# Decay matrices from exponentials of summed logarithms instead of scans, and a reordered pipeline, in a two-layer gated-delta kernel

## The chip, the cores and the metric

One core of a Trainium2 chip. Times are device microseconds of one execution; "before" was timed three times. The profile is of one more execution. TensorE does the matrix products and transposes, VectorE, ScalarE and GpSimd the elementwise work, and SyncE issues most of the DMAs. A pass of TensorE over f32 operands appears in the profile as two instruction records for one call in the kernel.

## The reference

Input: 8 sequences of 256 tokens with 128 features, f32. Layer 0 is a gated delta rule (16 value heads and 8 key heads of width 64) and a mixture of experts, layer 1 an attention and a mixture of experts. The change is in the first half of layer 0. Per sequence it computes (x is the normalised input):

```
mixed = silu(causal_conv4(x @ W_qkv.T));  q, k, v = split(mixed)      # q scaled by 1/8
z     = x @ W_z.T
beta  = sigmoid(x @ W_b.T)
g     = -exp(A_log) * softplus(x @ W_a.T + dt_bias)                    # log of the decay
for each token t, per head:
    S = S * exp(g_t)
    S = S + k_t (v_t - k_t S) beta_t
    o_t = q_t S
h = o * silu(z);  h = h * rsqrt(mean(h*h) + 1e-6) * norm_weight;  y = h @ W_out.T
```

The kernel works in chunks of 128 tokens. In a chunk the recurrence is a triangular system. Its matrix entry for the tokens i and j is (k_i . k_j) times beta times the product of the decays between them, so for each head and chunk a 128 x 128 matrix D of beta times products of decays is needed, 32 of them in a sequence.

## The kernel before, in words

The first layer runs as a software pipeline over `it` from -2 to 7. In one turn sequence f = it + 2 is normalised, projected and convolved; sequence n = it + 1 gets its matrices D, its products and the inverse of its triangular matrices; sequence i = it gets solutions, outputs, states, the norm of the heads and the output projection. Each engine's order is written out by hand in a loop of its own; engines wait on semaphores, and a queue never overtakes. After it comes a loop over four pairs of sequences for the rest (the mixture of experts and the second layer), which the diff does not touch apart from where the constants lie.

What the change touches:

- **D by scans.** `decays` (ScalarE, line 560) takes exponentials of the log decays. `decay_rows` (TensorE, line 950) spreads the decays of four heads along the rows of a PSUM bank, `diagonal` (GpSimd, line 454) puts beta on the diagonal of `dm`, and `scan` (VectorE, line 1586) multiplies and adds along 512 columns, so that `dm` becomes D. Batch k = 0 to 7 is four heads of one chunk. `w_last` copies D's last column.
- **Products.** `key_products` (TensorE, line 965) writes k.k and k.q of a batch to bank 2, and `products` (VectorE, lines 1604 and 1608) multiply them by D. The next batch's key products wait for `pt_ready` of the one before.
- **Decay to the chunk's end.** `turn_decay`, `gamma`, `turn_gamma` and `gamma_tokens` make the product of the decays from the chunk's start by a transpose, a scan and a transpose back.
- **Softplus.** `exponents` and `log_decays` (VectorE, lines 1534 to 1577) compute the log decay by a polynomial, in three parts. Beta is made by two instructions of its own from the same exponential.
- **The inverse.** `diagonal_blocks` (ScalarE, line 602) gathers the 32-row blocks, `invert` (VectorE, lines 1627 to 1641) inverts them in 30 steps of two instructions each, and then turns the result twice (1639 and 1641). TensorE merges the blocks to 64 rows and to 128 (`solve32`, `merge32`, lines 999 to 1015; `solve64`, line 1025; `merge64`, line 1038), with copies on ScalarE between them (lines 608 to 648).
- **Projection and convolution.** `project` (TensorE, line 935) computes a pair of channel tiles into banks 3 and 4 in turns, `seed` (ScalarE, line 571) starts the convolution of it, `convolve` (VectorE, line 1522) does six instructions, `silu` (ScalarE, line 580) ends it. A bank is free for the next pair but one when its convolution is done.
- **Gates.** `gate` (TensorE, line 920, ScalarE, line 668) computes z of sequence i and its Silu between the solutions and the outputs of that sequence.
- **Solutions, outputs, states.** `solve` (line 1057), `outputs` (line 1069), `end_state`, `from_state` (line 1090) on TensorE; `take_state`, `query_state`, `gated` on VectorE.
- **Norm of the heads.** `squares` (ScalarE, line 682), `sum_squares` (VectorE, lines 1664 and 1666), `root_of_squares` (GpSimd, line 468), `normalise` (VectorE, line 1670), then `turn_heads` (line 1106) and `project_out` (line 1118) on TensorE.

## Time and profile before

| | |
|---|---|
| median of three runs | 1913.48 us (1912.42 to 1915.88) |
| the profiled execution's own time | 1893.33 us |
| its span, first to last instruction | 1891.5 us |
| busy: TensorE, VectorE, ScalarE, GpSimd | 1473.5, 1000.2, 658.6, 196.7 us |
| mean granted clock of TensorE | 0.782 of full |
| sequence pipeline of layer 0 | to about 1037 us |

Engines overlap, so the busy times do not add up to the span. A share of busy time alone does not say which engine a stage waits for; for that the profile is cut into stretches. TensorE's granted clock has two levels here, 1.0 (2.4 GHz) and 0.5 (1.2 GHz); a mean between them says how much of the stretch was at either. The sections of the profile name engines in short: PE is TensorE, DVE VectorE, ACT ScalarE, POOL GpSimd.

### The profile page before, as it was taken

Reading aid. Unit: us, or ns where it says so; the run is one execution under the profiler, and the core shown is the slowest. Engines: PE = TensorE matmul, PEld = TensorE weight load, DVE = VectorE, ACT = ScalarE, POOL = GpSimd, SP = SyncE. Lnnn points to the kernel's source line nnn. Section 1 sums busy time; section 2 is a strip of 40 time slices with the busy share of each in tenths; the row PEclk is TensorE's granted clock in tenths of the full one; section 3 lists DMA queues with packets and bytes.
Section 4 is the critical chain, followed back from the end, with each engine's and each line's share of the span. In section 5 each row is a group of like instructions: output and inputs, shape, how many; then the busy total and the mean of one; then the engine's idle time right before and its main releaser. Section 6 shows DMA issues by size and latency. Waiting matters only on the chain.

```text
span 1891.5 us, 28271 instructions
## 1 busy us (share of the span) xinstructions
PE 1473.5 (78%) x11320; PEld 1115.6 (59%) x11328; DVE 1000.2 (53%) x2493; ACT 658.6 (35%) x1089; POOL 196.7 (10%) x189
## 2 busy tenths in 40 slices
PE   2759599597794995958857877897869977897879
PEld 1547487476674774757756554665547654566446
DVE  5866765867668567676742462225331452235421
ACT  1433252342522533425332413342333423342332
POOL 5010030200201202002001000000010000000010
PEclk8658667687586675966958877898789977898879
DMA  3000000000000000000003000000000000000000
GB/s 98 3 1 4 0 10 1 1 9 1 2 9 1 10 1 1 7 1 26 1 1 131 1 7 1 1 7 6 2 0 1 7 6 1 1 6 1 1 1 6
DMA packets 15078, 17.77 MB, mean 9 GB/s; under 512 B 2567, under 2 KB 13344, under 8 KB 14560
## 3 DMA queue, kind: packets, MB, share of 16 engines
q1 hardware_dynamic: 12768, 14.03, 2.2%
q8 instruction: 93, 1.52, 0.3%
q0 software_dynamic: 576, 1.76, 0.3%
q10 hardware_dynamic: 1600, 0.12, 0.1%
q14 instruction: 41, 0.34, 0.1%
HBM read 13.81 MB, written 2.10 MB: 8 GB/s over the span
## 4 chain that ended last, share of the span: by engine, by line
PE 41%; issue 29%; DVE 23%; ACT 3%; POOL 2%; DMA 1%; SPq 0%; DVEq 0%; POOLq 0%; ACTq 0%
DVE arena L1632 4%; DVE arena L1635 4%; PE ps L1069 4%; PE ps L1440 4%; PE ps L1449 3%; PE ps L965 3%; PE ps L935 3%; PE ps L1025 3%; PE ps L1038 3%; DVE arena L1522 3%; PE ps L950 2%; PE ps L920 2%; PE ps L1057 1%; PE ps L999 1%; PE ps L1257 1%
## 5 line engine op out<-in xcount | busy, mean ns | idle before, releaser
L1522 DVE SCALAR_TENSOR_TENSOR arena<-ps,conv_w,arena 128x255 f32<-128x255 f32 (+2 forms) x384 | 166.0, 476 | 108.0 <-ACT arena L571 103.4
L999 PE MATMUL ps<-arena 32*32 32x32 f32 x512 | 28.9, 236 | 156.7 <-DVE arena L1639 156.7
L1449 PEld LDWEIGHTS ps<-arena 128*128 128x128 f32 x1152 | 133.7, 192 | 15.3 <-issue 14.6
L1440 PE MATMUL ps<-arena 128*128 128x512 f32 x288 | 139.6, 633 | 0.0
L1449 PE MATMUL ps<-arena 128*128 128x128 f32 x1152 | 133.8, 275 | 0.0
L858 ACT ACTIVATE arena<-ps 128x512 f32<-128x512 f32 x144 | 86.0, 597 | 132.2 <-PE ps L1440 132.1
L1586 DVE TENSOR_TENSOR_SCAN arena<-ps,arena 128x512 f32<-128x512 f32 x64 | 78.1, 1220 | 99.2 <-PE ps L950 99.2
L999 PEld LDWEIGHTS ps<-arena 32*32 32x32 f32 x512 | 27.9, 151 | 158.5 <-DVE arena L1639 158.5
L935 PE MATMUL ps<-arena 128*128 128x256 f32 x256 | 104.0, 554 | 21.9 <-DVE arena L1522 21.3
L1930 DVE SCALAR_TENSOR_TENSOR arena<-ps,rw,arena 128x128 f32<-128x128 f32 x128 | 36.0, 344 | 139.0 <-PE ps L1449 139.0
L468 POOL TENSOR_TENSOR o_rstd<-ssq,half_power 128x16 f32<-128x16 f32 x16 | 46.4, 2901 | 562.9 <-DVE ssq L1666 562.9
L965 PE MATMUL ps<-arena 64*128 64x256 f32 x256 | 88.0, 473 | 17.4 <-DVE arena L1608 17.4
L494 POOL TENSOR_TENSOR rstd<-var_eps,half_power 128x2 f32<-128x2 f32 (+1 forms) x28 | 23.3, 833 | 746.6 <-DVE var_eps L1493 746.6
L1440 PEld LDWEIGHTS ps<-arena 128*128 128x128 f32 x288 | 56.4, 205 | 60.0 <-issue 59.0
L935 PEld LDWEIGHTS ps<-arena 128*128 128x128 f32 x256 | 64.6, 277 | 41.9 <-DVE arena L1522 28.7
L1635 DVE TENSOR_TENSOR arena<-arena 128x30 f32<-128x30 f32 (+14 forms) x240 | 79.7, 332 | 8.2
L1632 DVE TENSOR_TENSOR arena<-arena 128x30 f32<-128x30 f32 (+14 forms) x240 | 79.6, 332 | 8.2
L1069 PEld LDWEIGHTS ps<-arena 128*128 128x128 f32 x512 | 79.5, 248 | 5.2 <-issue 5.2
L1069 PE MATMUL ps<-arena 128*128 128x64 f32 x512 | 80.4, 332 | 0.0
L950 PE MATMUL ps<-con,decay 128*128 128x128 f32 x512 | 78.0, 304 | 2.8 <-DVE arena L1586 2.8
L950 PEld LDWEIGHTS ps<-con,decay 128*128 128x128 f32 x512 | 71.2, 212 | 10.6 <-issue 5.2
L1235 PE MATMUL ps<-con,h_tok 128*128 128x128 f32 x48 | 13.4, 434 | 82.0 <-DVE h_tok L1499 82.0
(247 smaller groups left out, 3139.3 us busy)
## 6 DMA issues: line engine op xcount, KB each, us to landing
arena<-in_routed_up SPq DMA_DIRECT2D x1, 2048.0 KB, 9.7
arena<-in_routed_down SPq DMA_DIRECT2D x1, 2048.0 KB, 14.7
x_ln<-in_x SPq DMA_DIRECT2D x8, 128.0 KB, 2.1
arena<-in_w_mix SPq DMA_DIRECT2D x1, 1024.0 KB, 10.4
x_in<-in_x SPq DMA_DIRECT2D x8, 128.0 KB, 2.6
out_x<-x_res SPq DMA_DIRECT2D x8, 128.0 KB, 1.9
arena<-out_x SPq DMA_DIRECT2D x4, 256.0 KB, 2.8
out_x<-arena SPq DMA_DIRECT2D x4, 256.0 KB, 2.7
```

The lines of the kernel that those rows point to most:

```text
L858: act.activation(hid1[e % 2][:, i, :], ps[:, i, :], ACT.Gelu).then_inc(s["mgelu"], 1)
L935: mm = pe.matmul(ps[:, 4 - p % 2, j * SEQ:(j + 1) * SEQ], w_mix[:, m * P:(m + 1) * P], hT3[:, f % 3, :], start=True, stop=True)
L950: mm = pe.matmul(ps[:, k % 2, h * P:(h + 1) * P], decay[n % 2][:, c, v:v + 1].to_broadcast([P, P]), ident0, start=True, stop=True)
L965: mm = pe.matmul(ps[:, 2, 2 * P * g:2 * P * (g + 1)].rearrange("p (q n) -> p q n", q=2), mix_qk[n % 2][r:r + DH, QK_TILES + m, cs], mix_qk ...
L999: pe.matmul(ps[32:64, c, BLOCK * h:BLOCK * (h + 1)], at[0:32, v, 32:64], tt[0:32, v, 0:32], start=True, stop=True)
L1069: mm = pe.matmul(ps[:, (7, 5)[g], h * DH:(h + 1) * DH], dm[i % 2][:, VH * c + v, :], eps[:, v, :], start=True, stop=True)
L1440: pe.matmul(ps[:, i, :], m_up[:, e, i * P:(i + 1) * P], hT, start=True, stop=True)\
L1449: mm = pe.matmul(ps[:, 4 + e % 2, c * P:(c + 1) * P], hid1[e % 2][:, i, c * P:(c + 1) * P], m_down[:, e, i, :], start=(i == 0), stop=(i == ...
L1522: ins = dve.scalar_tensor_tensor(conv_tile(f, m)[:, sh:SEQ], ps[:, 4 - p % 2, j * SEQ:(j + 1) * SEQ - sh], conv_w[:, m, TAPS - 1 - sh:TAPS ...
L1586: dve.tensor_tensor_scan(d, ps[:, k % 2, :], d, 0.0, ALU.mult, ALU.add).then_inc(s["scan_done"], 1)
L1632: me.did(dve.tensor_tensor(tmp, inv[:, j + 1:BLOCK, j:j + 1].to_broadcast([P, rows, j]), inv[:, j:j + 1, 0:j].to_broadcast([P, rows, j]), ...
L1635: me.did(dve.tensor_tensor(inv[:, j + 1:BLOCK, 0:j], inv[:, j + 1:BLOCK, 0:j], tmp, ALU.add))
```

## The change

Each matrix D is now the exponential of a sum of logarithms. `masked_decays` (GpSimd) multiplies the log decays of four heads into an upper triangle of ones. `decay_sums` (TensorE) puts the causal mask of large negative numbers into a PSUM bank with a bf16 matmul and adds the sums of the log decays with one f32 matmul of 512 columns. `decay_matrix` (ScalarE) takes the exponential of the bank, one instruction for each head, with the logarithm of beta as its per-partition bias, and writes D. The logarithm of beta comes from the same polynomial as softplus, whose tiles are twice as wide. The decay to the chunk's ends comes from three small matmuls (`chunk_ends`) and one exponential. Signs change in places, since D now has beta positive.

The order of every engine changes too. Five pairs are projected before the inverse ends, into banks 0 to 4. The gates move to the end of the turn and are computed for sequence n in bank 2. The second solve and outputs come after the last key products. The inverse is cut into three parts, with the gated outputs and a sum of squares between them. The first sum of squares and its normalise stand next to each other.

```diff
-                pool.tensor_tensor(dm[f % 2][:, BATCH * k:BATCH * (k + 1), :], over_heads(ident, BATCH),
-                                   over_last(beta[:, c, BATCH * b:BATCH * (b + 1)], P), ALU.mult)\
+                pool.tensor_tensor(gm[k % NB].rearrange("p (h n) -> p h n", h=BATCH), over_heads(upto, BATCH),
+                                   over_last(log_decay[n % 2][:, c, BATCH * b:BATCH * (b + 1)], P), ALU.mult)\
...
+            def decay_matrix(n, k):
...
+                act.wait_ge(s["sum_psum"], CH * NB * n + k + 1)
+                for h in range(BATCH):
+                    v = BATCH * b + h
+                    ins = act.activation(dm[n % 2][:, BATCH * k + h, :], ps[:, k % 2, h * P:(h + 1) * P], ACT.Exp,
+                                         bias=log_beta[n % 2][:, c, v:v + 1])
+                ins.then_inc(s["dm_ready"], 1)
...
-                for h in range(BATCH):
-                    v = BATCH * b + h
-                    mm = pe.matmul(ps[:, k % 2, h * P:(h + 1) * P], decay[n % 2][:, c, v:v + 1].to_broadcast([P, P]), ident0,
-                                   start=True, stop=True)
+            def decay_sums(n, k):
+                if k < 2:
+                    pe.wait_ge(s["conv_done"], NP * n + k + 1)
+                else:
+                    pe.wait_ge(s["dm_ready"], CH * NB * n + k - 1)
+                pe.matmul(ps[:, k % 2, :].rearrange("p (h n) -> p h n", h=BATCH), causal_bf[:, 0, :],
+                          over_heads(ident_bf[:, :], BATCH), start=True, stop=False, skip_group_check=True)
+                pe.wait_ge(s["gm_ready"], CH * NB * n + k + 1)
+                pe.matmul(ps[:, k % 2, :], beyond, gm[k % NB], start=False, stop=True, skip_group_check=True)\
+                    .then_inc(s["sum_psum"], 1)
...
+PAIR_BANK = (0, 1, 2, 4, 3, 4, 3, 4)
...
+                if p >= 5:
                     pe.wait_ge(s["conv_done"], NP * f + p - 1)
...
-                dve.tensor_tensor_scan(d, ps[:, k % 2, :], d, 0.0, ALU.mult, ALU.add).then_inc(s["scan_done"], 1)
...
+            for bank in LEVEL32:
+                for h in range(BATCH):
+                    pe.transpose(ps[:, bank, h * P:(h + 1) * P], ident, ident)
```

VectorE's order after the sixth batch of products, before and after (each name is one call above; i, n and f as in the text):

```diff
-  scan 7, products 6, sum_squares(i, 0), log_decays 1, products 7, gamma_tokens, log_decays 2,
-  normalise(i, 0), gated(i, 1, 0), gated(i, 1, 1), invert(n), sum_squares(i, 1), residual(i, 0),
-  convolve 0, 1, normalise(i, 1), convolve 2 to 6, residual(i, 1), convolve 7
+  log_decays 1, products 6, products 7, log_decays 2, sum_squares(i, 0), normalise(i, 0),
+  inverse steps to 13, gated(i, 1, 0), gated(i, 1, 1), steps 14 to 22, sum_squares(i, 1),
+  steps 23 to 30, turned_inverse, residual(i, 0),
+  convolve 0, 1, normalise(i, 1), convolve 2 to 6, residual(i, 1), convolve 7
```

TensorE's order from the last key products on, after the change: solve(i, 1), outputs(i, 1), the v and k transposes, turn_heads(i, 0), project 0 to 4, project_out(i, 0), solve32 and merge32, solve64 of two groups, project 5, solve64 of two groups, merge64, project 6, two of merge64, project 7, merge64, gate, decay_sums 0 and 1 of f, gate, turn_heads(i, 1), gate, project_out(i, 1), gate. ScalarE's queue ends with the gates' last two Silus, then the Silus of the four v pairs, and begins the next turn with decay_matrix 0 and 1.

## Rows read from the trace of the kernel before

**Rows 1.** The page's first line.

```profile
span 1891.5 us, 28271 instructions
```

**Rows 2.** Stretches by iteration; busy us of each engine (instructions), TensorE clock, DMA share, GB/s.

```profile
114.70:235.10 120.40, 92.22 (x813) 77.09 (x813) 82.69 (x190) 44.93 (x76) 14.00 (x14) 0.68 0.01 2
...
483.80:606.50 122.70, 94.64 (x836) 79.52 (x836) 85.90 (x196) 45.97 (x78) 17.77 (x15) 0.71 0.02 4
...
732.90:855.50 122.60, 94.64 (x836) 79.64 (x836) 85.87 (x196) 45.96 (x78) 17.76 (x15) 0.71 0.01 3
855.50:965.40 109.90, 83.04 (x822) 70.56 (x822) 80.55 (x165) 42.58 (x70) 17.14 (x14) 0.76 0.04 12
```

**Rows 3.** Stretches inside the iteration from 483.8 us: two cuts, same columns.

```profile
483.80:527.40 43.60, 41.53 (x556) 36.92 (x556) 29.41 (x66) 27.42 (x46) 14.83 (x14) 0.66 0.03 8
527.40:575.20 47.80, 44.09 (x232) 35.09 (x232) 27.53 (x56) 9.97 (x16) 2.94 (x2) 0.78 0.01 4
575.20:606.50 31.30, 9.03 (x48) 7.51 (x48) 28.96 (x78) 8.58 (x17) 0.00 (x0) 0.66 0.00 0
...
483.80:512.50 28.70, 28.62 (x468) 25.58 (x469) 17.76 (x36) 17.64 (x28) 11.87 (x9) 0.50 0.01 2
...
556.90:580.30 23.40, 20.85 (x82) 17.83 (x83) 12.59 (x31) 5.37 (x11) 2.90 (x1) 0.51 0.00 1
```

**Rows 4.** Waits from 483.8 to 606.5 us: total, times, longest.

```profile
DVE arena L1522 <- ACT arena L571: 13.3, 4, 4.6
```

**Rows 5.** Timeline of VectorE: start us, duration us, instruction.

```profile
483.71 1.89 DVE L1641 STREAM_TRANSPOSE arena<-arena 128x1024 f32<-128x1024 f32 x1
486.97 5.26 DVE L1522 SCALAR_TENSOR_TENSOR arena<-ps,conv_w,arena 128x255 f32<-128x255 f32 x12
524.27 1.22 DVE L1586 TENSOR_TENSOR_SCAN arena<-ps,arena 128x512 f32<-128x512 f32 x1
566.13 1.21 DVE L1664 TENSOR_REDUCE ssq<-arena 128x16 f32<-128x1024 f32 x1
576.53 1.22 DVE L1670 TENSOR_TENSOR arena<-arena,o_rstd 128x1024 f32<-128x1024 f32 x1
```

**Rows 6.** ScalarE's groups by form in the second layer: busy us, mean ns.

```profile
L858 ACT ACTIVATE arena<-ps 128x512 f32<-128x512 f32 x144 | 86.0, 597 | 132.2 <-PE ps L1440 132.1
L850 ACT ACTIVATE arena<-ps,a_b 128x512 f32<-128x512 f32 x16 | 11.0, 687 | 14.8 <-PE ps L1421 14.8
L814 ACT ACTIVATE arena<-ps 128x128 f32<-128x128 f32 x16 | 4.4, 278 | 18.3 <-PE ps L1292 18.3
```

**Rows 7.** Timeline of TensorE in the second layer, a bf16 matmul.

```profile
1754.72 0.63 PE L1321 MATMUL ps<-causal_bf,ident_bf 128*128 128x512 bf16 x1
```

**Rows 8.** Chain that ended last, TensorE's longest pieces: start, us, line, records.

```profile
491.04 2.00 PE ps L935 x4
493.05 5.31 PE ps L1025 x48
512.81 1.11 PE ps L935 x4
529.83 3.29 PE ps L920 x4
557.48 3.60 PE ps L1057 x16
564.89 7.02 PE ps L1069 x32
```

**Rows 9.** Line 468, the power: duration ns min/median/max, first and last start.

```profile
L468 POOL TENSOR_TENSOR o_rstd<-ssq,half_power x16: 2900/2901/2902, 196.1 to 1024.7; 128x16 f32<-128x16 f32 x16
```

**Rows 10.** Timeline of ScalarE around a load of the exponential table.

```profile
549.48 1.28 ACT L555 ACT_TABLE_LOAD   x1
550.78 0.26 ACT L555 ACTIVATE exp_out<-exp_in 128x64 f32<-128x64 f32 x1
```

**Rows 11.** Line 1560, the polynomial's steps: duration ns min/median/max.

```profile
L1560 DVE SCALAR_TENSOR_TENSOR sp_p<-sp_p,sp_z x48: 191/193/979, 27.4 to 818.3; 128x32 f32<-128x32 f32 x48
```

More of the change, by code:

```diff
@@ L479, in _ @@
                         weighted(i, b)
+                if has_n:
+                    for k in range(5, CH * NB):
+                        masked_decays(n, k)
+                if has_i:
                     root_of_squares(i, 0)
@@ L729, in _ @@
                     turned_heads(i, 0, 1)
+                if has_f:
+                    for p in range(5):
+                        seed(f, p)
+                if has_i:
                     squares(i, 1)
@@ L1064, in outputs @@
                     pe.wait_ge(s["e_ready"], 4 * i + 2 * c + g + 1)
+                    if c == 0 and g == 0:
+                        after(pe, "x_updated", CH * i)
                     if c == 1 and g == 0:
@@ L1719, in _ @@
                 if has_n:
-                    scan(me, n, 4)
                     products(me, n, 3)
```

511 lines of the change are left out of this document (250 added, 261 removed).

## The prediction

> **What bounds the kernel.** I read the page first: the profiled execution has a span of 1891.5 us [rows 1] and its own time is 1893.3 us, 20 us below the median of the three timed runs (1913.5 us). I sum differences in the profiled execution and take them off the median. The table of stretches cuts the first layer at the point where VectorE ends the transpose that releases the 32-row solve (line 1639). From the first such point (114.7 us) to the seventh (855.5 us) there are six full iterations, 123.5 us each, and one of 109.9 us that has no front part [rows 2]. Everything after about 1037 us is the second layer, which the diff leaves alone.
>
> No engine is full in the iteration from 483.8 to 606.5 us: TensorE is busy 94.6 us of 122.7, VectorE 85.9, ScalarE 46.0 [rows 2]. So I cut it into stages [rows 3]. Stage A (483.8 to 527.4, 43.6 us, to the first product of the next sequence) is TensorE's: busy 41.5 us, and its clock stands at the lower level (1.2 GHz, 0.50 of full) for the first 28.7 us. VectorE waits there 13.3 us, four times, for the projection and seed of the next pair [rows 4]. Stage B (527.4 to 575.2, 47.8 us, the eight batches of scans and products) is TensorE's too, busy 44.1 us, the stretch from 556.9 at half clock. Stage C (575.2 to 606.5, 31.3 us) is VectorE's inverse: VectorE 29.0 us busy, TensorE 9.0. The change fills the TensorE hole in C, which costs nothing now, and adds to VectorE there, where it costs.
>
> **The change, stage B.** The eight scans (1.22 us each [rows 5]) leave VectorE, but VectorE has slack in B (27.5 us of 47.8 [rows 3]); ScalarE's 32 exponentials replace them. Price of one: a 128-wide ACTIVATE from PSUM is 278 ns, a per-partition bias adds 90 ns (687 against 597) [rows 6], so 0.37 us; I let neighbours overlap by 0.1 us, which gives 1.2 us a batch, between 1.1 and 1.5 (no overlap). That is 9.6 us more on ScalarE, busy 10.0 us of 47.8: it fits. On TensorE a batch of decay rows (512 f32 columns) becomes 512 bf16 columns and 512 f32 columns; the f32 part is even and the bf16 part is 0.2 us, bounded by nothing and by the 0.63 us of such an instruction alone [rows 7]: six batches in B give +1.3 us. What leaves B counts more: the four gates (3.3 us for two, and two at 1.1), the second solve (3.6 us at half clock for one half, 1.8 for the other) and the second outputs (7.0 us) [rows 8], together 17.9 us, go after the last product or into stage A. One wait is new: products 6 and 7 stand next to each other and the key products share a bank, so the last one waits a product and two thirds of the softplus polynomial behind it, 2.8 us. B = 47.8 - 17.9 + 1.3 + 2.8 = 34.0 us. Bounds: with all of B at full clock 30 us; with a stretch of 24 us at half clock in it about 41.5 us.
>
> **Stage C.** On VectorE, from the last product to the released transpose, both sums of squares are now inside (the first was ahead of product 7, the second after the transpose): 2 x 1.3 us (reduce 1.21 [rows 5] and its scaling). The first is followed at once by the normalise, which needs GpSimd's power, 2.90 us [rows 9]; nothing stands between them, so VectorE waits 3.0 us and with it the inverse that is queued behind. Before, product 7 and the last decay steps covered this. Twice as wide log operations and two more settles: 0.3 us. C = 31.3 + 2.6 + 3.0 + 0.3 = 37.2 us. TensorE's second solve, outputs, transposes and five projections lie beside it: some 22 us at full and 33 us with half of it at the low clock, against 30 us until VectorE asks for the second squares (which ScalarE has queued behind the seeds of pairs 0 to 4). So nothing, up to 4 us if slow; I take nothing.
>
> **Stage A**, counted from the released transpose. VectorE turns the inverse back (1.9), adds one residual (0.3), convolves pairs 0 and 1 (5.26 for two), normalises (1.2) and convolves pairs 2 and 3 [rows 5]: 13.9 us. This is good: four conv waits are gone, since five pairs were projected early. But TensorE, after the 32-row blocks (7.2 us, the start of the first projection at 491.04) and two 64-row groups (5.31 us for three, so 1.77 each at half clock) [rows 8], is ready at 10.8 and its projection of pair 5 waits for pair 3's convolution: 3.1 us lost. Then 2.0 (pair 5), five groups (8.85) and two projections (4.0) bring it to 28.8; the last group and the first gate (2.0) to 32.6. I let the clock rise there, against 28.7 us before, as the wide matmuls come later. Then at full clock two decay sums (2.6), three gates (3.3), the heads' two transposes (2.2) and the output projection (2.2): 42.9. The next sequence's exponential comes later still, since ScalarE's queue holds in front of it the last gate's Silu (0.7), the four v Silus (2.3), which in the old order ran beside the convolutions, and a table load (1.28 [rows 10]); with the first batch of exponentials (1.2) this is 48.5 us. Before, it was 43.6: A = +4.9. VectorE has then been idle since about 34. If TensorE stays at half clock through A it is 57; if it is full from 20 us on it is near 43.
>
> **Sum.** 48.5 + 34.0 + 37.2 = 119.7 against 122.7: -3.0 us, six times -18. The iteration without a front part ran its middle at full clock already, so I give it nothing; likewise the last. In the start-up, the polynomial's six steps took up to 979 ns against 193 [rows 11] while GpSimd multiplied its diagonals; these multiplies now come after it: -6 us with their neighbours. Eight added identity transposes (half clock, 0.5 each, 1.5 of 4 hidden) and wider operations give 3 back, the rest of the start-up -1: -4 us. Together -22 us: 1913.5 - 22 = 1891.5, so 1892 us.
>
> **Two rules of the Trainium skill against it.** The load of the exponential table at 549.48 has no idle time of ScalarE before it, and the exponential starts 1.30 us after it began [rows 10]. The Trainium skill, ScalarE: Activation LUTs, section "What ACT_TABLE_LOAD costs", puts a drain of about 1.38 us beside the load's 1.28 us. By this rule A's queue would be 1.4 us longer in seven iterations, an estimate of 10 us from that page and 1902 us in all; the trace has no such gap. The Trainium skill, SBUF — State Buffer, section "Who interferes with whom", says that a VectorE instruction with two SBUF inputs and a GpSimd one that reads SBUF exclude each other; the 979 ns row agrees, and it is why GpSimd's multiplies 5 to 7, now in the front, could block state updates there. By it each block would cost up to 0.8 us, an estimate from the same row; by my order of the queues they meet products, which read PSUM, and I count nothing.
>
> **Rivals.** (1) The forecast: 0.40. Own range 1878 to 1905, almost all of it faster by over 0.2%.
> (2) The front stays at full clock: B 30.5 us, an iteration 116.2, 6 x -6.5 - 4 = -43: 1870 us. For it: the iteration without front part was at clock 0.76 over all, the others 0.68 to 0.71 [rows 2], with nearly the same front; the short solves leave the front. Against: pieces of half clock have come in all six. 0.24.
> (3) Slower: the stretch of half clock that begins at 556.9 now, mostly under work that moves to C, falls into the front. B is then 41.5, C 39.2 through the late squares, the iteration 129.2, +6.5 us. In four of six iterations: 26 - 6 - 4 = +16: 1930 us. It decides from B = 37.7 us, that is about 17 us of half clock in the front; before it was 20 of 47.8 [rows 3]. TensorE pays here because A has also grown: the front starts 5 us later. 0.26.
> (4) The gain in B is eaten exactly by the waits in C and A, so that the reorder does nothing (within 4 us of 1913.5). 0.06.
> (5) The drain rule above, 1902 us: 0.02, since the trace speaks against it.
> (6) TensorE idles in A as I wrote, but the clock rises early (A 43): 1860 us. 0.02.
>
> 0.2% (4 us) is about what this kernel's runs can tell from no change. Faster by more: 0.38 of (1) gives 0.36, (2) 0.24, and 0.01 of the rest, 0.61. Within: 0.08. Slower: 0.31. The range takes in (2), the clock bounds of A and B, and (3) at five of six: 1852 to 1940.
>
> **What the profile after should show.** Iterations of about 120 us. VectorE: no scan; a 3.0 us gap before the first normalise that waits for GpSimd's power; four conv waits of before gone, but 12 to 15 us idle between the last convolution and the first product, ended by ScalarE's exponential. TensorE: busy over 20 us of stage C, where it was 9.0; one gap of about 3 us before pair 5. ScalarE: batches of four ACTIVATEs of about 0.37 us, one table load between the last v Silu and the first of them. Start-up: first release near 110 us instead of 114.7. I am wrong if B is above 38 us, if a batch takes over 1.5 us, if the power's wait is hidden, or if TensorE's granted clock in A and B together moves by more than 0.1.

## The result and the profile after

The kernel after takes 1846.13 us (median of four runs, 1841.42 to 1851.51) against 1912.95 us for the kernel before on the same chip, a ratio of 0.9653 with the interval 0.9619 to 0.9687. That is 67 us less where the forecast had 22 less. The direction and most of the waits came as forecast; the size did not, and the time lies 6 us below the range. The profiled execution took 1841.42 us, against 1893.33 us for the profiled one of before, which lay 20 us below its own median; so the two traces differ by 52 us only. The loop behind the first layer, which the change leaves alone, also differs by chance: from TensorE's first instruction in it on (L1227 before, L1269 after) it took 846 us in the trace of before and 860 in that of after. So differences are compared stage by stage here.

The page's first line of the kernel after.

```profile
span 1839.6 us, 27803 instructions
```

The table of stretches of the kernel after, cut at the same release points as [rows 2] (VectorE ends the transpose that lets the 32-row solve go, here line 1654). Columns as there: length, busy time of TensorE, its weight loads, VectorE, ScalarE and GpSimd with instructions in brackets, then TensorE's clock.

```profile
105.60:221.30 115.70, 95.83 (x776) 76.01 (x776) 73.75 (x177) 53.85 (x108) 17.01 (x15) 0.69 0.01 2
...
562.10:674.70 112.60, 93.30 (x800) 75.09 (x800) 74.87 (x180) 54.56 (x110) 17.01 (x15) 0.71 0.02 5
...
787.30:895.20 107.90, 87.06 (x774) 69.52 (x774) 69.29 (x150) 50.14 (x98) 16.98 (x14) 0.71 0.04 12
```

From 105.6 to 787.3 us there are six full iterations, 113.6 us each in the mean, where before had 123.5. The first two took 115.6 us, the last four 112.6; where the iterations of a kernel repeat like these four they are called steady here. Six times 9.9 is 59 us. VectorE has 11 us less to do in an iteration and ScalarE 9 more; TensorE's busy time is only 1.3 us less than in [rows 2].

The same view for the stages of the iteration from 562.1 us, A, B and C as in [rows 3], and then for the parts of A and B at either clock level.

```profile
562.10:608.18 46.08, 42.80 (x533) 33.99 (x534) 24.51 (x60) 28.45 (x48) 5.78 (x6) 0.63 0.03 7
608.18:637.86 29.68, 26.43 (x148) 18.58 (x147) 18.87 (x41) 13.77 (x40) 5.40 (x7) 0.93 0.02 6
637.86:674.73 36.87, 24.07 (x123) 22.52 (x122) 31.52 (x82) 12.35 (x24) 5.83 (x2) 0.64 0.00 0
562.10:596.40 34.30, 31.80 (x466) 25.97 (x467) 20.89 (x46) 21.08 (x33) 4.08 (x4) 0.50 0.01 2
596.40:634.00 37.60, 34.03 (x203) 24.04 (x201) 20.80 (x51) 20.58 (x53) 7.11 (x9) 1.00 0.04 11
634.00:637.86 3.86, 3.39 (x11) 2.56 (x11) 1.70 (x4) 0.56 (x1) 0.00 (x0) 0.50 0.02 4
634.00:654.50 20.50, 20.03 (x88) 18.59 (x89) 14.33 (x38) 6.06 (x10) 2.90 (x1) 0.50 0.00 1
```

Against [rows 3], A grew by 2.5 us, B shrank by 18.1 and C grew by 5.5. The second stretch at half clock (1.2 GHz) starts 71.9 us behind the release point and lasts 20.5 us, but B is over at 75.8; 3.9 us of it fall on B. Before, the stretch began at 73.7 us (the 556.9 of [rows 3] is 0.6 us early) and took 17.7 us of B. B also held a short one of 3.4 us, which the steady iterations of after do not have:

```profile
530.20:533.60 3.40, 3.40 (x8) 1.54 (x7) 1.46 (x4) 1.04 (x2) 0.00 (x0) 0.50 0.14 41
557.50:575.20 17.70, 17.45 (x68) 15.04 (x68) 7.13 (x18) 1.13 (x2) 2.90 (x1) 0.50 0.00 1
```

The waits of the iteration from 562.1 us of the kernel after (waiting engine and line, who released it: total us, times, longest).

```profile
DVE x_res L1694 <- PE ps L1166: 13.9, 1, 13.9
PE ps L1038 <- DVE arena L1654: 12.1, 1, 12.1
...
PE ps L1002 <- DVE arena L1634: 3.3, 1, 3.3
...
DVE arena L1686 <- POOL o_rstd L472: 3.0, 1, 3.0
...
PE ps L971 <- DVE arena L1564: 1.1, 1, 1.1
```

The first normalise waits 3.0 us for GpSimd's power, the last key product 3.3 us for products 6, and pair 5 only 1.1 us. VectorE is idle for 13.9 us in A, but ahead of its last residual; the last convolution is queued behind that. TensorE still has a hole of 12.1 us in front of the 32-row solve.

The timeline of ScalarE at the end of A (start us, duration us, instruction).

```profile
602.95 0.60 ACT L691 ACTIVATE arena<-ps 128x512 f32<-128x512 f32 x1 [2.17 <-PE ps L951]
603.45 2.19 ACT L602 ACTIVATE arena<-arena 128x512 f32<-128x512 f32 x4
605.66 1.28 ACT L572 ACT_TABLE_LOAD   x1
606.95 2.17 ACT L572 ACTIVATE arena<-ps,log_beta 128x128 f32<-128x128 f32 x8
```

The last gate's Silu, the four v Silus, the table load and the exponentials follow one another without a gap, and the first product starts at 608.18. The groups of the same iteration by form give the exponential's price.

```profile
L572 ACT ACTIVATE arena<-ps,log_beta 128x128 f32<-128x128 f32 x32 | 9.1, 381 | 5.2 <-PE ps L986 5.2
```

The start-up has its step too: the row of the polynomial, now twice as wide, takes its 0.22 us every time, where [rows 11] had up to 979 ns.

```profile
L1599 DVE SCALAR_TENSOR_TENSOR sp_p<-sp_p,sp_z x48: 224/225/226, 26.6 to 745.6; 128x64 f32<-128x64 f32 x48
```

### The profile page after: what moved, and what is told of

It is laid out like the page before. It is cut to its first block, busy times and chain, and to the rows that moved or that the text cites. A ratio compares the mean times of both kernels' runs of the same rounds, so it can differ in the third digit from the quotient of the medians.

```text
span 1839.6 us, 27803 instructions
## 1 busy us (share of the span) xinstructions
PE 1487.5 (81%) x11040; PEld 1097.3 (60%) x11048; DVE 909.1 (49%) x2365; ACT 730.9 (40%) x1347; POOL 193.3 (11%) x188
## 4 chain that ended last, share of the span: by engine, by line
PE 37%; issue 30%; DVE 25%; ACT 4%; POOL 3%; DMA 1%; SPq 0%; POOLq 0%; DVEq 0%; ACTq 0%
DVE arena L1564 5%; DVE arena L1645 4%; DVE arena L1648 4%; PE ps L1482 4%; PE ps L1491 3%; PE ps L1078 3%; PE ps L1002 3%; PE ps L986 3%; PE ps L971 2%; PE ps L1098 2%; PE ps L951 2%; PE ps L1112 2%; PE ps L1065 2%; PE ps L1463 1%; PE ps L1299 1%
## 5 line engine op out<-in xcount | busy, mean ns | idle before, releaser
L1491 PEld LDWEIGHTS ps<-arena 128*128 128x128 f32 x1152 | 133.7, 192 | 15.3 <-issue 14.6
L1482 PE MATMUL ps<-arena 128*128 128x512 f32 x288 | 135.3, 616 | 0.0
L971 PE MATMUL ps<-arena 128*128 128x256 f32 x256 | 89.0, 505 | 22.0 <-DVE arena L1564 21.3
L1002 PE MATMUL ps<-arena 64*128 64x256 f32 x256 | 79.4, 434 | 30.4 <-DVE arena L1634 24.8
L1002 PEld LDWEIGHTS ps<-arena 64*128 64x128 f32 x256 | 46.7, 203 | 83.0 <-DVE arena L1634 41.5
L1632 DVE TENSOR_TENSOR arena<-ps,arena 128x512 f32<-128x512 f32 x64 | 44.1, 690 | 105.3 <-PE ps L1002 76.3
L1098 PEld LDWEIGHTS ps<-arena 128*128 128x128 f32 x512 | 87.9, 271 | 7.6 <-issue 7.2
L1098 PE MATMUL ps<-arena 128*128 128x64 f32 x512 | 90.4, 359 | 0.2 <-DVE arena L1706 0.2
L572 ACT ACTIVATE arena<-ps,log_beta 128x128 f32<-128x128 f32 x256 | 72.4, 377 | 42.5 <-PE ps L986 42.2
L1482 PEld LDWEIGHTS ps<-arena 128*128 128x128 f32 x288 | 55.0, 200 | 57.0 <-issue 57.0
L1112 PE MATMUL ps<-arena 128*128 128x64 f32 x512 | 86.5, 349 | 0.0
L1112 PEld LDWEIGHTS ps<-arena 128*128 128x128 f32 x512 | 84.8, 262 | 2.3 <-issue 2.3
```

Source lines behind the costliest of these rows:

```text
L572: ins = act.activation(dm[n % 2][:, BATCH * k + h, :], ps[:, k % 2, h * P:(h + 1) * P], ACT.Exp, bias=log_beta[n % 2][:, c, v:v + 1])
L971: mm = pe.matmul(ps[:, PAIR_BANK[p], j * SEQ:(j + 1) * SEQ], w_mix[:, m * P:(m + 1) * P], hT3[:, f % 3, :], start=True, stop=True)
L1002: mm = pe.matmul(ps[:, 2, 2 * P * g:2 * P * (g + 1)].rearrange("p (q n) -> p q n", q=2), mix_qk[n % 2][r:r + DH, QK_TILES + m, cs], mix_qk ...
L1098: mm = pe.matmul(ps[:, 5 + g, h * DH:(h + 1) * DH], um[:, VH * c + v, :], v_tok[:, c, v, :], start=True, stop=True)
L1112: mm = pe.matmul(ps[:, (7, 5)[g], h * DH:(h + 1) * DH], dm[i % 2][:, VH * c + v, :], eps[:, v, :], start=True, stop=True)
L1482: pe.matmul(ps[:, i, :], m_up[:, e, i * P:(i + 1) * P], hT, start=True, stop=True)\
```

## The experiments

Fifteen kernels were run behind it, one of them the kernel after once more. The ratio is to the kernel before on the same chip. The ratios carry 0.3 to 0.9% to either side, so the mean length of the six full iterations in the trace (release point to release point) is what the theories are judged by. That mean has a spread of its own: the kernel after gave 113.6 us in one trace and 112.6 in the other, since a short stretch at half clock, 40 to 51 us behind the release point, lengthens some iterations by about 3 us, two of six in the first trace and one in the second. So a difference of 1 us between means shows nothing. A, B and C are those of the steady iterations, in us.

```
kernel                 ratio (interval)          iteration   A          B          C
before                 1                         123.5       42.8-45.9  46.3-49.2  31.3
after                  0.9653 (0.9619, 0.9687)   113.6       46.1       29.7       36.8
order_alone            0.9736 (0.9649, 0.9824)   115.1       45.2-46.5  31.8-35.1  36.7
filler_before_products 0.9767 (0.9688, 0.9847)   115.2       45.0-46.6  32.4-35.3  36.8
late_pairs             0.9701 (0.9610, 0.9791)   112.1       42.7       32.9       36.9
power_hidden           0.9583 (0.9501, 0.9664)   109.4       46.0       29.7       33.6
keep_busy              0.9663 (0.9583, 0.9742)   112.3       46.1       29.7       36.9
silus_early            0.9654 (0.9585, 0.9723)   112.7       44.0       31.7       36.9
power_silus_keep       0.9582 (0.9503, 0.9661)   111.0       44.0       31.7-35.0  33.6
before_keep_busy       1.0058 (1.0021, 1.0096)   123.3       42.8-45.4  45.8-49.2  31.3
solve_in_front         0.9771 (0.9724, 0.9817)   115.6       46.5       32.7       36.8
power_gates            0.9475 (0.9433, 0.9516)   109.5       43.8       28.8       36.8
power_gates_silus      0.9495 (0.9454, 0.9536)   108.8       41.3       31.2       36.7
after_again            0.9619 (0.9572, 0.9666)   112.6       46.1       29.7       36.8
before_solve_late      0.9657 (0.9601, 0.9713)   112.3       43.8-44.8  37.3       31.1
power_gates_squares    0.9375 (0.9338, 0.9412)   106.1       43.3-44.3  28.7-29.3  33.6
all_squares            0.9388 (0.9352, 0.9425)   106.4       41.1-41.9  30.8-31.4  33.6
```

**order_alone.** The new order of all engines, with the scans, the diagonals and the decay transposes of before in place of the exponentials.

```diff
-                    decay_sums(n, 2)
+                    decay_rows(n, 2)
...
-                    decay_matrix(n, 2)
...
+                    scan(me, n, 2)
                     products(me, n, 2)
```

> The changed kernel's order of all engines, with the scans, GpSimd's diagonals and the decay transposes of the kernel before in place of the exponentials. Theory 1 (the reorder makes the gain: the gates, the second solve and the second outputs leave TensorE's front, and the stretch of half clock then falls where TensorE is not waited for; VectorE has room for scans): an iteration of 114 to 117 us, in all 1850 to 1875 us. Theory 2 (the scans, 8 times 1.22 us, are the gain, since 9.8 us is what an iteration lost): 121 to 123 us an iteration, in all 1900 to 1915 us.

The first line of the diff is TensorE's, the next ScalarE's, the last VectorE's; it is the same for every batch. By the means the order has 8.4 of the 9.9 us per iteration and the exponentials 1.5; against the repeat of after it is 2.5, and the steady iterations are 115.0 to 117.0 us here against 112.6. Theory 1 holds; the exponentials' share lies between 1.5 and 4 us and is not known better.

**filler_before_products.** The kernel after with a reduce of 1.2 us, whose result nobody reads, on VectorE before each of the eight products.

```diff
+                me.did(dve.tensor_reduce(filler[:, :], w_out[:, :, :].rearrange("p m (a d) -> p (m a) d", d=DH), X_AXIS, ALU.add))
                 dve.wait_ge(s["kk_psum"], CH * NB * n + k + 1)
```

> The changed kernel with one reduce of 1.2 us on VectorE ahead of each batch of products (its result is not used), so that VectorE has the scans' time back and nothing else changes. Theory 1 (VectorE waits for TensorE in the front and can hide most of it): iteration 114 to 118 us, stage B at most 34 us. Theory 2 (VectorE's time is the path): iteration 122 us, stage B 39 us.

Some 9.8 us of VectorE's time put back cost 1.6 us of the iteration by the means, 2.6 against the repeat of after. Most of VectorE's load in the front is free, in agreement with order_alone.

**late_pairs.** Pairs 2 to 4 projected and seeded between the inverse's merges, as before the change.

```diff
-                    for p in range(5):
+                    for p in range(2):
                         project(f, p, n, has_n)
...
                     merge32(n, 1)
+                    project(f, 2, n, has_n)
                     solve64(i, n, 0, 0, has_i)
+                    project(f, 3, n, has_n)
                     solve64(i, n, 0, 1, has_i)
+                    project(f, 4, n, has_n)
```

These are TensorE's lines; ScalarE's seeds of the three pairs move with them.

> The changed kernel with pairs 2, 3 and 4 projected and seeded after the inverse again, between the blocks' solves. Theory 1: stage A grows by TensorE's three projections at half clock, 6 us, and by renewed waits for seeds; iteration 118 to 121 us, stage C unchanged. Rival (early projection gains nothing because TensorE's tail is bound by the last gates and VectorE is idle 14 us there anyway): iteration 113 to 115 us.

Theory 1 missed: the iteration is not longer. Two stretches of this kernel in A, from 10 to 18 and 18 to 26 us behind a release point at 333.9 us:

```profile
344.00:352.00 8.00, 8.00 (x42) 5.99 (x41) 5.23 (x12) 5.14 (x9) 0.48 (x1) 0.50 0.00 0
352.00:360.00 8.00, 8.00 (x89) 6.69 (x88) 5.13 (x12) 5.84 (x10) 0.00 (x0) 0.84 0.01 2
```

Here the clock rises to full (2.4 GHz) 20 to 21 us behind the release point, 14 us earlier than in the kernel after; it drops to half for 7 us from 41 us on, and B is longer by what A is shorter: A and B together are 75.6 us, against 75.8. That is so in three of the six iterations. In one the clock rose only 38 us behind the release point, and A and B together took 82.7 us (the iteration 119.5); in another the drop did not come, and they took 72.3 us (109.2). So 75.7 us is no fixed length: it moves with the clock.

**power_hidden.** The first normalise behind the fifth step of the inverse.

```diff
                     sum_squares(me, i, 0)
-                    normalise(i, 0)
-                    steps_of_inverse(me, n, 0, 14)
+                    steps_of_inverse(me, n, 0, 5)
+                    normalise(i, 0)
+                    steps_of_inverse(me, n, 5, 14)
```

> The changed kernel with the first normalise four inverse steps later, so that GpSimd's power runs beside VectorE. If stage C is VectorE's alone, as read: 3.0 us less in each of seven iterations, C 33.8 us, 21 us in all (1825 us). Rival (something else of C ends as late, TensorE's heads or projections): less than 1 us an iteration.

C falls to 33.6 us and the steady iteration by 3.3: the wait for the power (3.0 us) was on the path with its full length. VectorE sets C.

**keep_busy** and **before_keep_busy.** Nine and eighteen matmuls whose result nobody reads, in TensorE's hole before the 32-row solve, in the kernel after and in the kernel before.

```diff
+                if c == 0 and has_i:
+                    pe.wait_ge(s["hz_ready"], 4 * (i + 1))
+                    for _ in range(9):
+                        pe.matmul(ps[:, 5, :], ident, w_z[:, 0:512], start=True, stop=True)
...
-                    pe.wait_ge(s["hz_ready"], 4 * i + 3 + c)
```

The kernel before has 18 of them, into bank 7, and no change of a wait.

> The kernel after, with nine f32 matmuls of 128x512 whose result nobody reads put in front of the 32-row solve, where TensorE is idle for 12.1 us before the release point. Theory 1 (what TensorE does in the 12 us before the solve decides the clock behind it): the stretch at half clock in A, 33 us now, ends at least 10 us earlier; A falls from 46 us to 36 to 40, the iteration from 113.6 to 104 to 108, the kernel to about 1800 us. Rival (the many small matmuls of the 32-row and 64-row steps leave the clock low by themselves, whatever came before): A stays at 45 to 47 us with a clock of about 0.63, the iteration at 113 to 114; if the nine matmuls themselves run at half clock they take 15 us instead of 8 and push the solve back, the iteration is then 116 to 117.

> The kernel before, with eighteen f32 matmuls of 128x512 whose result nobody reads put in front of the 32-row solve, where TensorE is idle for 19.6 us before the release point. Theory 1 (what TensorE does before the solve decides the clock behind it): A's 28.7 us at half clock become shorter by 10 us or more, and A falls from 43.6 to about 36; the stretch at half clock in B may come earlier as well. If B keeps its 20 us at half clock the iteration goes from 123.5 to about 116. Rival (the small matmuls themselves leave the clock low): A stays at 43 to 44 us, and the iteration at 122 to 124; if the added matmuls run at half clock, they take 31 us and push the solve back by some 11 us.

In keep_busy, A of the iteration from 670.7 us, the last 12.7 us of that iteration, and TensorE's wait in them (the iterations before and behind it repeat to 0.1 us):

```profile
670.70:716.80 46.10, 42.62 (x533) 33.77 (x533) 24.54 (x59) 28.41 (x48) 5.79 (x6) 0.63 0.03 7
...
770.70:783.40 12.70, 8.37 (x24) 3.72 (x23) 11.78 (x32) 0.69 (x1) 2.93 (x1) 1.00 0.00 0
...
PE ps L1039 <- DVE arena L1655: 4.4, 1, 4.4
```

The nine matmuls ran at full clock, but they ended 4.4 us before the release point, and TensorE was idle from there to the solve (3.7 us in the kernel before, ahead of the release at 610.6 us). The clock fell 0.3 us behind the release point, and A is as long and its clock as low (0.63) as without. The rival holds in both kernels as far as they go; what they leave open, an idle time right before the solve, is closed by power_silus_keep below. The kernel before was 0.6% slower with its matmuls, though its iterations were not longer (123.3 us against 123.5).

**silus_early.** The Silus of the v pairs between the gates' Silus, VectorE's last residual behind its last convolution.

```diff
-                    silu(f, 2)
-                    silu(f, 3)
+                    for p in range(2, NP - 1):
+                        silu(f, p)
                     gate(n, 0, 1)
...
+                    silu(f, NP - 1)
                     gate(n, 1, 1)
-                    for p in range(QK_TILES, NP):
-                        silu(f, p)
```

> The kernel after, with the Silus of the v pairs put between the gates' Silus in ScalarE's queue instead of behind the last gate's, and VectorE's last residual behind its last convolution. Theory 1 (the front opens when ScalarE has worked off four v Silus behind the last gate, 2.3 us): A falls by about 2 us to 44, the iteration from 113.6 to about 111.5. Rival (TensorE's gates and output projection end A and the clock decides when, so ScalarE's queue is beside it): A stays at 46 us and the iteration between 113 and 114.5.

```profile
564.40:608.40 44.00, 40.48 (x514) 31.72 (x514) 24.63 (x59) 28.38 (x48) 5.78 (x6) 0.61 0.03 8
608.40:640.10 31.70, 28.45 (x167) 20.61 (x166) 18.76 (x40) 14.04 (x40) 5.45 (x7) 0.94 0.02 5
```

Neither text was right. The front opens 2.1 us earlier, as theory 1 says, but B is 2.0 us longer. Against the rows of after, 2.3 us of TensorE's busy time have gone from A to B, and the two stages together are 75.7 and 75.8 us. The clock rose and fell at the same points as in after (34.4 and 72.0 us behind the release point). So with the clock as it is, A plus B has one length, TensorE's, and ScalarE's queue at its boundary sets only where the cut lies.

**power_silus_keep.** The three edits power_hidden, silus_early and keep_busy together.

> The kernel after, with three edits together: the first normalise behind the fifth step of the inverse (3 us less in C by the run that did it alone), the v Silus and the last residual as in silus_early, and the nine idle-time matmuls of keep_busy. If the three add up as theory 1 of each says (3.2 + 2 + 6 to 9 us per iteration), the iteration is about 101 us and the kernel about 1770 us. By the rivals of the other two only the first counts: iteration 109.4 us and 1815 to 1825 us.

Not even the power's 3.2 us come through here: C is 33.6 us, but four of six iterations are still 112.5 to 112.7 us. Between 44.5 and 50.5 us behind the release point at 446.5 the clock was at half again.

```profile
480.70:490.50 9.80, 9.02 (x50) 6.07 (x50) 1.17 (x8) 6.96 (x16) 1.71 (x2) 1.00 0.09 27
491.00:497.00 6.00, 6.00 (x21) 4.41 (x21) 1.23 (x4) 1.79 (x6) 3.06 (x5) 0.50 0.09 25
```

This kernel also settles what keep_busy left open, since its C is shorter. Around the release point at 333.9 us:

```profile
321.00:333.90 12.90, 11.74 (x45) 6.83 (x43) 11.97 (x32) 3.98 (x9) 2.93 (x1) 1.00 0.00 0
333.90:340.80 6.90, 5.14 (x333) 5.02 (x334) 6.76 (x14) 4.69 (x8) 2.68 (x3) 0.99 0.02 5
340.80:368.00 27.20, 22.80 (x136) 17.24 (x135) 16.89 (x38) 16.68 (x27) 2.38 (x2) 0.50 0.00 1
```

TensorE is idle only 1.2 us before the solve. The clock stays full for the first 6.9 us of A (every second iteration has 3.3 to 3.5 instead), then falls while TensorE works on the 32-row and 64-row groups, and rises 34.2 us behind the release point, where it rises in silus_early too; A is 44.0 us in both. So TensorE's work before the solve moves the fall by a few microseconds, and neither the rise nor the length of A.

**solve_in_front.** The kernel after with the second solve and outputs, and ScalarE's copies, at their places of before.

```diff
+                    solve(i, 1)
                     decay_sums(n, 7)
                     key_products(n, 6)
+                    outputs(i, 1)
                     key_products(n, 7)
-                    solve(i, 1)
-                    outputs(i, 1)
```

> The kernel after, with the second solve and the second outputs (10.6 us of TensorE at half clock, 7 at full) and ScalarE's two copies between them put back to their places of before, ahead of the last two key products. Theory 1 (A and B together are TensorE's work, and it matters which work the stretch at half clock, from 71 us behind the release point on, falls on): the moved work meets that stretch inside the front, so B grows by 8 to 11 us, from 29.7 to 38 to 41, C stays at 36 to 37 because VectorE's inverse sets it, and the iteration is 121 to 124 us, all of the per-iteration gain gone. Rival (the forecast's way of counting: the moved work is worth its own length in the front, and the clock's share stays with the front wherever it is): that is 8 to 10 us too, but the half-clock share of B must then be as large after the move out as before it; the clock of B would be 0.78 in both, where the kernel after has 0.93. Rival 2 (ScalarE's exponentials and VectorE's products pace the front, TensorE has room): B 30 to 33 us.

Theory 1 falls. B came out in the range of rival 2 (30 to 33 us), but TensorE has no room in it: it is busy for 32.42 of the 32.70 us. A and B of this kernel, and the start of the second stretch at half clock:

```profile
455.20:501.70 46.50, 43.06 (x533) 34.00 (x534) 24.52 (x60) 28.47 (x48) 6.49 (x6) 0.62 0.03 7
501.70:534.40 32.70, 32.42 (x213) 24.79 (x212) 18.91 (x41) 14.95 (x42) 5.41 (x7) 1.00 0.02 5
...
538.50:549.00 10.50, 7.88 (x25) 6.14 (x26) 8.15 (x20) 3.87 (x8) 1.70 (x1) 0.53 0.00 0
```

The stretch started 83 us behind the release point here, so all of B ran at full clock; and the moved work also filled the 3.3 us in which TensorE waits for products 6. B grew by 3.0 us and the steady iteration by 3.4 (2.0 in the mean of six). In the new order these 7 us of full-clock work are worth a third of what they are worth in the old one (below).

**before_solve_late.** The counterpart: one part of the new order in the kernel before. The second solve and outputs go behind the last key products, and the gated outputs of the second chunk into the inverse. The scans, the gates and the late projections stay.

```diff
-                    solve(i, 1)
                     decay_rows(n, 7)
                     key_products(n, 6)
-                    outputs(i, 1)
                     key_products(n, 7)
+                    solve(i, 1)
+                    outputs(i, 1)
...
                     normalise(i, 0)
+                    invert(me, n, 0, 14)
                     gated(me, i, 1, 0)
                     gated(me, i, 1, 1)
-                    invert(me, n)
+                    invert(me, n, 14, BLOCK - 1)
```

> The kernel before with one part of the new order: the second solve and second outputs behind the last key products, ScalarE's copies of the solutions behind the last diagonal blocks, and the gated outputs of the second chunk behind step 14 of the inverse. Scans, gates, projections and everything else as before. The forecast's way of counting (what is moved leaves B with the length it has in the trace of before, 10.6 us at half clock, and the new wait for the last key product, 2.8 us, comes in; the half clock of the rest stays): B 40 us instead of 47.8, C 31 to 33, the iteration 116 us. Theory 1 (the stretch at half clock starts where it did, about 73 us behind the release point, and with less work in front of it the front is nearly over by then, so it also takes the half clock of the remaining work out of B): B 36 to 37 us and the iteration 112 to 113. Rival (the stretch moves forward with the work, since it follows the work TensorE has done at full clock and not the time): B 42 to 44 us and the iteration 119 to 121.

```profile
568.60:613.20 44.60, 41.49 (x556) 36.88 (x556) 29.39 (x65) 27.40 (x46) 14.83 (x14) 0.66 0.03 8
613.20:650.50 37.30, 31.32 (x178) 23.44 (x179) 27.28 (x57) 8.83 (x14) 2.92 (x2) 0.90 0.01 4
650.50:681.60 31.10, 19.41 (x104) 17.97 (x103) 28.80 (x77) 9.84 (x19) 0.00 (x0) 0.66 0.00 1
...
646.70:650.50 3.80, 3.80 (x17) 3.15 (x16) 3.49 (x15) 0.58 (x1) 2.90 (x1) 0.50 0.00 0
```

This one edit has the whole gain, 0.9657 against the full change's 0.9653. B is 37.3 us, A and C are untouched (C's TensorE is busy 19.4 us now instead of 9.0, and still waits 10.5 us for VectorE before the next solve). Of the long stretch at half clock only 3.8 us fall on B; the short one, 3.4 us from 47 us on, is there as before. Theory 1's iteration was met (112.3 us) and its B nearly (37.3 against 36 to 37), though by a stretch that begins at 78 us and not at 73. The waits of TensorE in this B:

```profile
PE ps L965 <- DVE arena L1606: 5.6, 3, 3.2
PE ps L920 <- ACT arena L668: 0.7, 1, 0.7
PE ps L1090 <- DVE arena L1689: 0.4, 1, 0.4
```

**power_gates, power_gates_silus.** power_hidden, with the first two gates moved from A into TensorE's hole in C (then also silus_early).

```diff
                     turn_heads(i, n, 0, 1, has_n)
+                    gate(n, 0, 0)
+                    gate(n, 0, 1)
...
                     merge64(n, 1, 1)
-                    gate(n, 0, 0)
                     decay_sums(f, 0)
                     decay_sums(f, 1)
-                    gate(n, 0, 1)
```

> The kernel after with the first normalise behind the fifth step of the inverse, and the first two of the four gates moved from TensorE's work in A into its idle time at the end of C. Theory 1 (A and B are TensorE's work, 75.7 us together): the two gates take 2.2 us out of A at full clock and cost nothing in C, so A plus B is about 73.5 us and the iteration 107 us, against 109.4 with the power alone. Rival (the clock takes back what is taken out, as it did with the v Silus: the iteration snaps to 112.6 us): 109 to 112.6 us.

> power_gates with the v Silus and the last residual as in silus_early. Theory 1 (TensorE sets A plus B, so an earlier opening of the front moves time from A to B and no more): A 2 us shorter and B 2 us longer than in power_gates, the iteration within 1 us of it. Rival (with less work for TensorE in A, ScalarE's queue is the next bound): 2 us less per iteration than power_gates, about 105 us.

A plus B falls from 75.8 to 72.5 us in both, but C is back at 36.8. The trace of power_gates names why: in C, VectorE waits for ScalarE's second Square, which is queued behind the gates' Silus and the seeds.

```profile
DVE ssq L1681 <- ACT arena L705: 3.1, 1, 3.1
```

**power_gates_squares, all_squares.** The same two with that Square ahead of the five seeds.

```diff
+                    squares(i, 1)
                     for p in range(5):
                         seed(f, p)
-                    squares(i, 1)
```

> power_gates with ScalarE's second Square moved in front of the seeds of pairs 0 to 4; in power_gates VectorE waits 3.1 us in C for it. If that wait is the whole loss of C (36.8 us against 33.6 with the power alone), C is 33.6 again, A plus B stays at 72.5 us, the iteration is 106.1 us and the kernel about 1790 us. Rival (the clock gives less back when C is shorter, as in power_silus_keep, where B grew by 5 us when C and A shrank by 5): the iteration stays at 109 us.

> power_gates_squares with the v Silus and the last residual as in silus_early. If TensorE sets A plus B: A 2.5 us shorter, B 2.5 longer, the iteration within 1 us of power_gates_squares. Rival (less work in A leaves ScalarE's queue as the bound): 2 us less per iteration.

```profile
530.50:636.70 106.20, 91.20 (x800) 73.58 (x800) 74.71 (x179) 54.13 (x110) 17.01 (x15) 0.76 0.02 5
530.50:574.10 43.60, 40.09 (x530) 33.04 (x531) 24.63 (x59) 26.22 (x46) 5.78 (x6) 0.62 0.03 8
574.10:603.00 28.90, 25.64 (x147) 17.93 (x146) 18.68 (x41) 13.58 (x40) 5.41 (x7) 0.96 0.02 6
603.00:636.70 33.70, 25.47 (x127) 22.61 (x127) 31.40 (x82) 14.33 (x27) 5.83 (x2) 0.75 0.00 1
```

This version takes 1786.92 us (1785.27 to 1799.57), 0.9375 of before (0.9338 to 0.9412): 3% faster than the kernel after. The lost 3.1 us were the Square's and not the clock's. With the v Silus early as well, A is 2 us shorter and B 2 us longer again, and the iteration is the same.

**after_again.** The kernel after, unchanged.

> The kernel after once more, unchanged, to see what its trace repeats and what not. If the start-up's 105.6 us to the first release point belong to the change, they come again within 1 us; if the kernels of the same start-up code (109.5, 109.7, 113.8, 114.9 and 115.1 us so far) differ by the clock's chance at the beginning, this one lies between 105 and 116 us too. Steady iterations should be 112.6 us again.

Steady iterations repeat to 0.1 us. The start-up does not: the first release came at 115.3 us, against 105.6. Over the thirteen traces with the new start-up code the mean is 111.5 us (105.6 to 117.0), over the four with the scans' code 117.9 (114.6 to 120.3).

## Why the prediction was wrong in size

**What held.** The mechanism did: work leaves the front for a stage that VectorE sets. Of the rivals, (2) came nearest in B (30.5 us; its iteration is 116.2); (6) lies nearer in time (1860 us), but by an A of 43 us, which did not come. C was forecast at 37.2 us and is 36.8; the power's wait was forecast at 3.0 and is 3.0, and power_hidden shows that it is paid in full. The new wait for the last key product was forecast at 2.8 us and is 3.3. A batch of exponentials was priced at 1.2 us, 0.37 each; one takes 381 ns on the mean and four take 1.21. The start-up was forecast at 4 us less and is some 6 less by the means above; the 9 us between the two profiled executions are partly chance. Rival (3), half clock moved into the front, did not come: the second half-clock stretch takes 3.9 us of B where it took 17.7. None of the forecast's four signs of being wrong came: a batch takes 1.21 us, the power's wait is paid, and TensorE's clock over A and B together went from 0.72 to 0.75. For B they had a bound on the slow side alone, so they could not tell of this miss.

**The step that failed is the working of stage B**, "47.8 - 17.9 + 1.3 + 2.8 = 34.0 us"; measured 29.7. The subtraction treats all that is left as unchanged. TensorE was busy 44.1 us of B and idle 3.7 [rows 3]. Left over, by the sum, are 44.1 - 17.9 + 1.3 = 27.5 us busy and 3.7 + 2.8 = 6.5 us idle. The trace of after has 26.4 busy and 3.3 idle. So 1.1 us of the error is in TensorE's busy time and 3.2 us in waits of TensorE that I carried along. The 1.1 us are a net, by an estimate from the durations of the instructions: the work that stayed in B was busy 7.3 us at half clock in before, and TensorE is busy 3.4 us at half clock in B of after, which makes about 2 us less; the work itself is about 1 us more than the sum has. These were the waits in the front of the kernel before:

```profile
PE ps L965 <- DVE arena L1608: 2.0, 1, 2.0
PE ps L1057 <- DVE arena L1696: 1.1, 1, 1.1
PE ps L920 <- ACT arena L668: 0.7, 1, 0.7
PE ps L1090 <- DVE arena L1688: 0.4, 1, 0.4
```

One waits for products that stand behind a scan, the others stand at the work that is moved. Not one of them is in the trace of after, whose only wait of TensorE in B is the new one. The runs separate the parts. Moving the second solve and outputs was worth 5.4 + 7.0 us of work less 2.8 of the new wait by my prices, which gives 38.2 us for B; before_solve_late has 37.3 (its expectation, 40, left out the 1.8 us of the second solve that ran at full clock, so it told less against the forecast's counting than it said). The rest of the change in B (gates out, decay sums in, scans gone) was counted 4.2 us and brings 7.6 us, from 37.3 to 29.7. Of the difference, 3.4 us, 2.7 are TensorE's idle time, 6.0 us in before_solve_late's B and 3.3 in after's; the other 0.7 are in its busy time. "VectorE has slack in B" was true of its busy time and not of each wait. Put back with the order kept, the scans cost 1.5 us per iteration by the means (order_alone).

**Stage A**, forecast 48.5 us, is 46.1. Pair 5 waited 1.1 us and not 3.1. The order of ScalarE's queue at the end was as forecast, and silus_early shows that the v Silus, 2.2 us, do hold the first product. What the forecast did not see is that this wait is not worth its length: TensorE goes on with work of B or finishes work of A while the cut moves, and A plus B stays 75.7 us. The clock's rise was forecast at 32.6 us behind the release point and came at 34.3.

**The baseline.** The stages were taken from an iteration of 122.7 us, and six of them average 123.5 [rows 2]; the change also brings the mean nearer to its steady value. Per iteration this makes 2.4 (A) + 4.3 (B) + 0.4 (C) = 7.1 us more than the forecast's 3.0, which is the steady 112.6 against 122.7; the two longer first iterations of after and the longer ones of before about cancel, and the mean gain is 9.9 us. Six times 9.9, 2.0 of the iteration without a front part (109.9 to 107.9) and 6 of the start-up are 67 us; the end of the first layer behind the last release gives 4.6 us back (75.0 to 79.6), as the second chunk's solve now lies there in the open. Forecast were 18, 0, 4 and 0. Forecast and measured terms sum to 22 and 63 us; the medians differ by 67.

**Where the gain is from.** before_solve_late takes 11.2 us off the iteration; everything else of the change together adds 1.3 (113.6 against 112.3), or nothing on the steady ones: 7.6 us less in B, 5.7 more in C and 2 more in A. Each of the two lengths hangs on where the stretches at half clock fall, so that they agree this well may be chance; no run tests it. More than half of C's share was avoidable, as power_hidden shows.

**The rules of the Trainium skill.** The load at 605.66 lasts 1.28 us and the exponential starts at 606.95, at once behind a Silu that ends at 605.64. The drain of about 1.38 us that the Trainium skill, ScalarE: Activation LUTs, section "What ACT_TABLE_LOAD costs" puts beside the load is not in this trace either, so rival (5) is out. In the start-up, the six wide steps take 224 to 226 ns in every iteration now that GpSimd's multiplies start at 29.8 us, behind them; up to 979 ns was seen beside them. The exclusion of VectorE and GpSimd in the Trainium skill, SBUF — State Buffer, section "Who interferes with whom", agrees with both figures.

**What stays open** is what starts the second stretch at half clock. It began 74 us behind the release point in before, 72 in after, 78 in before_solve_late and 83 in solve_in_front. A short one of 3 to 10 us, mostly from 40 to 48 us on, came in before, before_solve_late, late_pairs and power_silus_keep, and in some iterations of after and not in others of the same trace. Where it falls on the front, the iteration is about 3 us longer: after has 115.6 with it and 112.6 without, power_silus_keep 112.6 and 109.3. In after and silus_early the clock had been full for 37 to 38 us when it fell. The share at full clock is nearly the same over an iteration of before and after (0.71 in both), which fits with a clock that takes back elsewhere what it gives, but that was not tested; keep_busy has 0.76 with matmuls added, so it is no fixed share.

## What to carry to other kernels

When work leaves a stage, do not subtract its length and keep the rest: list the waits that stood in the stage, and ask of each whether it goes too. The end of one stage and the start of the next may only be a cut in the work of the engine that runs through both; add both lengths before an earlier start is counted as a gain, and look whether the clock stayed the same. Move work into a hole of its engine, then look which queue it stands in front of: two gates moved into TensorE's hole paid only after ScalarE's Square had been taken from behind their Silus.

## What the runs showed of the hardware

- The many 32-row and 64-row matmuls behind the release point run at half clock with TensorE busy 31.8 of 34.3 us (after, clock 0.50). Where TensorE had been busy 11.74 of 12.9 us at full clock before them (power_silus_keep), the clock fell 6.9 us into them and rose at the same point as without. Where wide projections stand among them (late_pairs), the clock rose 14 us earlier in four of six iterations, and later in one.
- In before, after and before_solve_late a stretch at half clock of 17 to 24 us came in every full iteration although TensorE had been busy over 80% of the time ahead of it (34.03 of 37.6 us in after, 21.74 of 23.9 us in before).
- The same kernel, run again, gave steady iterations equal to 0.1 us, a mean of six that differed by 1.0 us and a start-up that differed by 10 us.
